# One gather in 4 KB rows, a bounce through DRAM, and free loading at the head of a mixture-of-experts kernel

## What is computed

```python
# x (32, 64, 512), itok (32,), cond_weights (200, 64, 64), E = 8 experts, I = 352
w  = cond_weights[itok]                       # one 64 x 64 matrix per batch entry
xf = einsum('bct,bcd->bdt', x, w).reshape(2048, 512)
gate = softmax(xf @ Wr.T)                     # (2048, 8)
# the two best experts of each row; an expert keeps its first 640 rows
g = silu(xf @ Wg[e].T); u = xf @ Wu[e].T; out_e = (g * u) @ Wd[e].T
y = sum over the two experts of gate * out_e
result = x + y
```

## Time and profile before

| | us |
|---|---|
| median of 3 runs | 307.38 (306.9 to 308.51) |
| the profiled execution, its own time | 307.83 |
| its span in the trace | 306.0 |
| PE busy | 281.3 (92%) |
| DVE, ACT, POOL busy | 134.4, 125.7, 139.1 |

### The profile page before, as it was taken

The page is one execution under the profiler, slowest core; times in us unless marked ns, Lnnn a source line. Parts: engine busy times, 40 slices in busy tenths (PEclk is TensorE's granted clock), DMA queues, the critical chain, the costliest instruction groups (busy, mean ns, idle before and its releaser), DMA issues.

```text
span 306.0 us, 4658 instructions
## 1 busy us (share of the span) xinstructions
PE 281.3 (92%) x1626; PEld 248.0 (81%) x1627; DVE 134.4 (44%) x259; ACT 125.7 (41%) x212; POOL 139.1 (45%) x128
## 2 busy tenths in 40 slices
PE   2899898799989999999999999999999999999940
PEld 2576366699879999999999999999999999999930
DVE  2377895434334344543444355354335534423200
ACT  2132675243334435534354354444435445432220
POOL 5773087500374343545444436454753553454230
PEclk9999995999999999999999999999999999999995
DMA  4855693979796867578658675795879666474422
GB/s 155 277 182 154 249 383 104 327 293 403 266 170 150 215 148 174 163 180 152 149 90 229 131 176 170 161 165 150 238 158 208 157 132 103 69 138 47 58 37 35
DMA packets 24992, 53.17 MB, mean 174 GB/s; under 512 B 3344, under 2 KB 3344, under 8 KB 24976
## 3 DMA queue, kind: packets, MB, share of 16 engines
q0 software_dynamic: 9472, 21.67, 37.4%
q1 hardware_dynamic: 15504, 31.29, 30.7%
HBM read 32.69 MB, written 20.25 MB: 173 GB/s over the span
## 4 chain that ended last, share of the span: by engine, by line
PE 75%; DMA 10%; POOL 5%; DVE 3%; issue 2%; SPq 2%; POOLq 1%; ACT 0%; DVEq 0%
PE bank L853 39%; PE bank L873 21%; PE bank L836 4%; DMA out<-x_sb 4%; DMA tiles<-xf_dram,src_row 4%; PE bank L897 3%; POOL whi L399 3%; PE bank L736 3%; PE bank L748 2%; DMA x_sb<-x 2%; POOL tiles L412 1%; SPq L344 1%; PE bank L771 1%; PE bank L780 1%; PE bank L758 1%
## 5 line engine op out<-in xcount | busy, mean ns | idle before, releaser
L412 POOL DMA_INDIRECT tiles<-xf_dram,src_row x40 | 44.3, 1107 | 95.4 <-ACT tiles L504 65.7
L424 POOL DMA_INDIRECT out<-tiles,dst_row x40 | 66.2, 1654 | 43.7 <-DMA out<-tiles,dst_row 20.1
L853 PE MATMUL bank<-whi,xhi 128*128 128x352 f32 x280 | 73.4, 343 | 0.8 <-ACT xhi L488 0.8
L853 PE MATMUL bank<-wlo,xhi 128*128 128x352 f32 x280 | 67.9, 323 | 0.0
L853 PE MATMUL bank<-whi,xlo 128*128 128x352 f32 x280 | 56.8, 324 | 0.0
L853 PEld LDWEIGHTS bank<-wlo,xhi 128*128 128x128 f32 x280 | 48.8, 188 | 0.0
L696 DVE TENSOR_TENSOR xlo<-bank,xhi 128x512 fp32r<-128x512 f32 x35 | 24.2, 691 | 55.8 <-ACT xhi L488 55.8
L853 PEld LDWEIGHTS bank<-whi,xlo 128*128 128x128 f32 x280 | 47.0, 189 | 0.0
L853 PEld LDWEIGHTS bank<-whi,xhi 128*128 128x128 f32 x280 | 45.7, 189 | 1.2 <-issue 1.2
L488 ACT ACTIVATE xhi<-bank 128x512 fp32r<-128x512 f32 x35 | 21.0, 599 | 61.0 <-PE bank L836 61.0
L873 PE MATMUL bank<-whi,hhi 128*128 128x512 f32 x105 | 41.4, 395 | 1.4 <-DVE hlo L720 1.4
(11 more groups left out here) (92 smaller groups left out, 248.0 us busy)
## 6 DMA issues: line engine op xcount, KB each, us to landing
raw<-wgu SPq DMA_DIRECT2D x32, 352.0 KB, 3.8
x_sb<-x SPq DMA_DIRECT2D x8, 512.0 KB, 4.2
raw<-wd SPq DMA_DIRECT2D x8, 512.0 KB, 3.8
out<-x_sb SPq DMA_DIRECT2D x4, 1024.0 KB, 7.5
xf_dram<-tiles SPq DMA_DIRECT2D x7, 520.0 KB, 4.0
raw<-wd SPq DMA_DIRECT2D x8, 192.0 KB, 5.1
out<-x_sb SPq DMA_DIRECT2D x1, 1280.0 KB, 13.3
tiles<-xf_dram,src_row POOLq DMA_INDIRECT x40, 4.7
```

Of the source, the lines that this page charges most:

```text
L412: nc.gpsimd.indirect_dma_start(out=xg[:, n % TPE, :], out_offset=None, in_=xf_dram[:, :], in_offset=bass.IndirectOffsetOnAxis(ap=src_row[: ...
L424: nc.gpsimd.indirect_dma_start(out=out[:, :], in_=y_sb[:, n % TPE, :], in_offset=None, out_offset=bass.IndirectOffsetOnAxis(ap=dst_row[:, ...
L853: last = nc.tensor.matmul(ps[:, 0:I], left[:, b, c], right[:, half, o:o + I], start=(k == 0 and left is xhi and right is whi), stop=(k == ...
```

## The change

The condition matrices come in one indirect DMA: each 64 x 64 matrix is seen as four rows of 4 KB, a partition takes one of the 128 rows, and DVE makes one column of row numbers. Since the rows land in another layout than the blocks need, ACT's queue writes them to a scratch tensor in DRAM (`wsel_dram`) and reads them back into both diagonal blocks of `wbd` with two DMAs of 64 x 16 pieces of 256 bytes. The copies on DVE and ACT into `wbd` go away. The wait between the loads of x goes away, the router's weights come padded to 32 columns from the host (64 KB, no memset before), and the first expert's weights wait for no gather. PE begins with ten 128x512 bf16 matmuls on zeros. All logits now stand ahead of all wide products; ACT takes tile 15's copy too, and does three copies of xf before its second exponential. Two of the four 1 MB pieces of the initial copy to `out` are issued early.

```diff
@@ SP
-            for half in range(2):
-                sp.dma_start(condb[half * C:(half + 1) * C, :],
-                             cond[half:half + 1, :].broadcast_to([C, TT])).then_inc(cond_in, 16)
             load_x(0)
-            sp.wait_ge(wr_clear, 1)
-            sp.dma_start(wr_sb[:, :, 0:E],
-                         wr.rearrange("(k p) e -> p k e", p=P)).then_inc(wr_in, 16)
+            sp.dma_start(wr_sb[:, :, :], wr[:, :, :]).then_inc(wr_in, 16)
             for m in range(1, TT // 2):
-                if m >= 2:
-                    sp.wait_ge(x_in[m - 2], 16)
                 load_x(m)
...
-            sp.wait_ge(wc_in[NG - 1], 16 * GR)
             sp.wait_ge(pad_ok, 1)
             for u in range(NU):
                 load_unit(0, u)
+            def init_out(q):
+                for m in range(q * XR // 2, (q + 1) * XR // 2):
+                    sp.wait_ge(x_in[m], 16)
+                sp.dma_start(out_t[:, q * XR:(q + 1) * XR, :],
+                             x_sb[:, q * XR:(q + 1) * XR, :]).then_inc(out_init, 16)
+            for q in range(EARLY_OUT):          # EARLY_OUT = 2
+                init_out(q)
...
-            for m in range(TT // 2):
-                sp.wait_ge(x_in[m], 16)
-            for q in range(TT // XR):
-                sp.dma_start(out_t[...], x_sb[...]).then_inc(out_init, 16)
+            for q in range(EARLY_OUT, TT // XR):
+                init_out(q)
@@ POOL
             pool.wait_ge(cidx_ok, 1)
-            for j in range(TT):
-                nc.gpsimd.indirect_dma_start(
-                    out=wc_sb[:, j, :], out_offset=None, in_=wcond[:, :],
-                    in_offset=bass.IndirectOffsetOnAxis(ap=cidx[:, j:j + 1], axis=0),
-                ).then_inc(wc_in[j // GR], 16)
+            nc.gpsimd.indirect_dma_start(
+                out=wsel_sb[:, :], out_offset=None, in_=wcond[:, :],
+                in_offset=bass.IndirectOffsetOnAxis(ap=cidx[:, 0:1], axis=0),
+            ).then_inc(wsel_in, 16)
@@ ACT
-            for j in range(0, TT, 2):
+            act.dma_start(condb[:, :], cond[:, :]).then_inc(cond_in, 16)
+            for j in TURN_ACT:                  # the even tiles and 15
                 act.wait_ge(tT_ps, j + 1)
                 nc.scalar.activation(tT_sb[...], ps_tT[j % XR][...], ACT.Copy)
+                if j == SENT_AT:                # 2
+                    act.wait_ge(wsel_in, 16)
+                    act.dma_start(wsel_dram.rearrange("b (q e) -> (b q) e", q=CQ),
+                                  wsel_sb[:, :]).then_inc(wsel_out, 16)
+                if j == BACK_AT:                # 6
+                    act.wait_ge(wbd_clear, 1)
+                    act.wait_ge(wsel_out, 16)
+                    wsel_t = wsel_dram.rearrange("(j t) (c d) -> t c j d", t=2, d=D)
+                    for t in range(2):
+                        act.dma_start(wbd[t * C:(t + 1) * C, :, t * D:(t + 1) * D],
+                                      wsel_t[t]).then_inc(wbd_in, 16)
             exps(0)
...
-            xf_copy(0, 0)
+            for n in range(XR - 1):
+                xf_copy(n, n)
             exps(1)
-            for n in range(1, XR):
-                xf_copy(n, n)
+            xf_copy(XR - 1, XR - 1)
@@ PE
+            pe.wait_ge(warm_clear, 1)
+            for _ in range(WARM_UP):            # 10
+                nc.tensor.matmul(ps_lg[0][:, :], warm[:, 0:P], warm[:, :], start=True, stop=True)
             pe.wait_ge(consts, IDENT)
...
             def logits(g):
                 pe.wait_ge(xr_ok, g + 1)
-                if g < NG - 1:
-                    pe.wait_ge(wbd_ok, 2 * (g + 1))
-                else:
-                    pe.wait_ge(wbd_last_ok, 2)
+                pe.wait_ge(wbd_in, 32)
```

More of the change, by code:

```diff
@@ L93, in build @@
         carry = sb("carry", [P, E, A])
-        condb = sb("condb", [P, TT], I32)
-        cidx = sb("cidx", [P, TT], U32)
-        wc_sb = sb("wc_sb", [P, TT, D])
+        condb = sb("condb", [P, 1], I32)
+        row_i = sb("row_i", [P, 1], I32)
+        part_i = sb("part_i", [P, 1], I32)
+        part = sb("part", [P, 1])
+        cidx = sb("cidx", [P, 1], U32)
+        wsel_sb = sb("wsel_sb", [P, CP * D])
+        warm = sb("warm", [P, H], BF16)
         wbd = sb("wbd", [P, TT, 2 * D])
@@ L219, in build @@
         out_t = out[0:N, :].rearrange("(j p) h -> p j h", p=P)
+        TURN_ACT = [j for j in range(TT) if j % 2 == 0 or j == TT - 1]
+        TURN_DVE = [j for j in range(TT) if j not in TURN_ACT]
         def tile(i, s):
@@ L357, in _ @@
         def _(pool):
[L359 to L365, removed]
+            nc.gpsimd.iota(row_i[:, :], [[0, 1]], base=0,
+                           channel_multiplier=1).then_inc(consts, 1)
             nc.gpsimd.memset(ident[:, :], 0.0).then_inc(consts, 1)
-            pool.wait_ge(consts, 3)
+            pool.wait_ge(consts, 2)
             nc.gpsimd.affine_select(out=ident[:, :], in_=ident[:, :], compare_op=ALU.not_equal,
@@ L530, in _ @@
         def _(dve):
[L531 to L535, removed]
+            nc.vector.memset(warm[:, :], 0.0).then_inc(warm_clear, 1)
+            dve.wait_ge(consts, 1)
+            nc.vector.tensor_scalar(part_i[:, :], row_i[:, :], CQ - 1, None,
+                                    ALU.bitwise_and).then_inc(part_ok, 1)
+            dve.wait_ge(part_ok, 1)
+            nc.vector.tensor_copy(part[:, :], part_i[:, :]).then_inc(part_ok, 1)
+            dve.wait_ge(part_ok, 2)
+            dve.wait_ge(cond_in, 16)
+            nc.vector.tensor_scalar(cidx[:, :], condb[:, :], float(CQ), part[:, :], ALU.mult,
                                     ALU.add).then_inc(cidx_ok, 1)
             nc.vector.memset(wbd[:, :, :], 0.0).then_inc(wbd_clear, 1)
[L539 to L548, removed]
+            nc.vector.memset(raw[IR:P, DOWN + (KI - 1) * H:WC], 0.0).then_inc(pad_ok, 1)
             chain = [0]
@@ L567, in gates @@
                                         ALU.subtract).then_inc(sub_ok, 1)
+            def gates(h):
+                js = slice(h * HALF, (h + 1) * HALF)
+                wide = [P, HALF, E]
                 dve.wait_ge(ex_ok, h + 1)
@@ L728, in _, with turned @@
         def _(pe):
+            def turned(j):
+                if j in TURN_ACT:
+                    pe.wait_ge(tT_act_ok, TURN_ACT.index(j) + 1)
+                else:
+                    pe.wait_ge(tT_dve_ok, TURN_DVE.index(j) + 1)
             def x_tile_turn(j):
@@ L740, in router @@
             def router(g):
-                pe.wait_ge(tT_even_ok, (g + 1) * (GR // 2))
-                pe.wait_ge(tT_odd_ok, (g + 1) * (GR // 2))
+                for j in range(g * GR, (g + 1) * GR):
+                    turned(j)
                 if g >= 1:
@@ L791, in _ @@
                     x_tile_turn((g + 1) * GR + 1)
+                else:
+                    logits(0)
                 router(g)
@@ L795, in _ @@
                     x_tile_turn((g + 1) * GR + 3)
-                if g == NG - 1:
-                    logits(0)
+                else:
+                    logits(1)
                 turn(g)
-            for g in range(1, NG):
+            for g in range(2, NG):
                 logits(g)
-                condition(g - 1)
-            for j in range(NG - 1, BEFORE_RANKS):
+            for j in range(BEFORE_RANKS):
                 condition(j)
```

73 lines of the change are left out of this document (37 added, 36 removed).

## The result

| | before | changed |
|---|---|---|
| median of 4 runs each, one chip | 307.88 us (306.9 to 308.51) | 322.41 us (322.3 to 323.92) |
| profiled execution, its span | 307.83, 306.0 | 322.3, 320.5 |

The ratio is 1.0494 (1.0451 to 1.0537): the change makes the kernel 4.9% slower, 14.5 us. The forecast was 304.2.

The account below looks back on a forecast made before the run. The prediction took only the start of DVE's second half of gates and one PE stall to move the end: 307.83 - 1.5 (head) - 1.7 (stall) = 304.6, or 304.2 for the median, range 301.3 to 308.0.

Parts of the forecast that it names:

- the second sum: DVE's sum after the second exponential in the head: predicted at L + 8.7, 29.7 us, against 31.23 before.
- the matrices' path: Head: condition numbers, gather, write to scratch, reload; predicted to have the matrices in place at 21.0 us.
- The exponential behind the copies of xf: Head, on ACT: second exponential waits for three copies of xf, predicted to lose 1.4 us.
- The stall: Expert loop: PE's single wait for POOL's sixth gather, behind the initial output copy; all 1.7 us predicted to go.
- L: Time at which PE can start its first logits, the later of two paths; predicted 21, so the head gains 1.5 us.
- fair shares: Rival for the head's transfers, chance 0.20: gather gets half the engines beside x; L = 18.7, time 301.9.
- L to the second sum: Head, from PE's first logits to DVE's sum after the second exponential: predicted 8.7 us.
- the fourth rival: Lower clock over the expert loop's first tile, chance 0.07: about 3 us at half speed, 1.5 lost, time 305.7.
- ACT's DMAs behind SP's backlog: Rival, chance 0.10: queues served in issue order, write and reload each pay 5.4 us more; L = 30, time 313.
- Late matrices: Rival, chance 0.18: gather, write and reload each take the upper price; L = 24.3, time 307.4, no change.
- the main case: The prediction's own sum, chance 0.45: L from 19.5 to 22.5, time from 302.8 to 305.8.
- POOL's 15 other gathers: Head: removing them was predicted to be worth nothing, since they do not stand in the chain.

Follow-up runs that it names:

- b_held: Changed kernel with SP's first weights and early output held until the reload has landed: 308.95 us, ratio 0.967 to the kernel before.
- m_held_again: b_held run again unchanged in the fourth set: 308.96 us, ratio 0.965 to the kernel before.
- after_again: The changed kernel run again unchanged in the second set, on another chip: 321.02 us, ratio 1.003 to the kernel before.
- n_after_third: The changed kernel run again unchanged in the fourth set: 321.95 us, ratio 1.008 to the kernel before.
- h_cond: b_held with the condition numbers issued first on SP's queue instead of on ACT's: 310.62 us, ratio 0.972 to the kernel before.
- f_filled: Changed kernel with 16 and 24 bf16 matmuls on zeros in PE's waits before tile 12's turn and the first logits: 315.78 us, ratio 0.987 to before.
- g_gathers: b_held with 13 more indirect gathers on POOL behind the needed one, into an unread buffer: 318.53 us, ratio 0.997 to the kernel before.
- d_free: Kernel before with x loads unpaced, weights not waiting for the gathers and two output pieces early: 318.53 us, ratio 0.998 to the kernel before.
- before_again: The kernel before run again unchanged in the second set, on another chip: 319.19 us, ratio 1.000.

## Why the prediction was wrong

**What held.** The kernel is bound where the prediction said: the second sum is 14.8 us later than in the earlier trace rows, the end 14.5, and nearly all of it was there before the expert loop. The order of the matrices' path, reload last with PE's first logits right behind it, is that of the chain. The exponential behind the copies of xf costs what was said, 1.4: from the first logits to the second sum are 8.60 us in b_held (24.59 to 33.19) and 7.24 in i_exps (22.97 to 30.21). The stall of the earlier trace rows went, all 1.7 of it. It went with room to spare. POOL's sixth gather in the changed kernel still waits for the output:

```profile
89.48 0.94 POOL L415 DMA_INDIRECT tiles<-xf_dram,src_row  x1 [17.37 <-DMA out<-x_sb]
```

But it lands 3.3 us later, and PE turns its tile only at 100.53. Counted from PE's first tile of the loop it goes out after 20.1 us, before after 27.5: 7.4 us earlier, where the prediction had some 6.

**The step that failed first: the matrices' path to L.** Term by term, with what each measured:

| term | predicted | measured | off |
|---|---|---|---|
| gather issued | 3.8 | 5.84 | +2.0 |
| gather | 7.0 | 7.35 | +0.4 |
| write | 5.0 | 6.15 | +1.2 |
| ACT's two issues, to the second | 0.5 | 0.76 | +0.3 |
| reload, its second DMA | 4.7 | 10.90 | +6.2 |
| L | 21.0 | 31.16 | +10.1 |

The reload was mis-sized. I took 4.7 between an old gather and a 260 KB gather, and priced its small pieces as 2.0 us of data while busy. That price is enough when nothing else is queued: 3.7 and 3.6 us in b_held and m_held_again. It is wrong beside SP's queue, for two reasons that the windows show. No piece of the reload moves before 23.5, 4.1 us after the first of its DMAs was issued (1.5 in b_held, 17.43 to 18.9); the cause of this is open. And from then to 28 the price of a piece is not its own bytes but the 2 KB piece of the other queue that goes between. My reading of the earlier trace rows, 3.6 us for an old gather beside the loads of x, hid this: those gathers ran while SP was paced and held at most two loads ahead. It is the row of another queue's state. The rule of the Trainium skill that the prediction used for fair shares ("DMA: Bandwidth & Descriptors", section "Queues, rings and completion order": engines take the queues in turn, packet by packet) fits the window of 24 to 26 us, 345 against 345, and those of after_again and n_after_third, 352 against 351 and 354 against 348; it does not explain the wait to 23.5. Such counts can't tell how many pieces a turn holds. Where I erred was to make of equal turns equal bytes: the bytes of two pieces are as 1 to 8.

The condition load has the same mistake in small: 4.4 us for 128 pieces of 4 bytes, issued together with 512 KB of x, against the 2.4 of the earlier trace rows, measured when SP had issued it first. In h_cond, first in the queue, it is 2.0 again. But the time saved there is lost in gather and write, so its 2.0 us are in the sum and not in what could be gained.

**The step that failed second: L to the second sum.** Predicted 8.7, measured 14.9. f_filled measures 8.6 with the same order and the same late reload, so the order was right, and what I left out is the clock: 6.2 us to the prediction's 8.7, 6.3 to f_filled. (The order was sized with luck: the prediction's L + 5.2 for the last logits doesn't follow from its own prices, which give 5.45; b_held has 5.1.) The prediction took the full clock in the head for granted once the warm-up had run, and considered the lower one only around the lists. Waits of PE of 3.4 to 3.8 us in the head, which the prediction had at 1 to 2 us, stand ahead of both stretches at 0.50. The clock fell again over the loop's first tiles, as the fourth rival had it, in this window of the changed kernel from 70 to 90:

```profile
70.00:90.00 20.00, 18.11 (x102) 17.21 (x103) 7.48 (x10) 5.93 (x12) 2.32 (x3) 0.91 0.94 340
```

A mean of 0.91 over 20 us is 3.6 us at 0.50, if the rest is at 1.00; the stretch lies at 71.5 to 74.9. What remains for it in the sum below is about 1.0 us; no run took it apart.

**The sum as it came out.** L is 10.1 later than predicted, the way to the sum 6.2 longer: second sum at 46.05 instead of 29.7, and 14.8 behind the earlier trace rows. From there to the loop 0.8 more than before (23.3 against 22.5; the wait for the first gather is 1.6, before 0.8), the first tile 1.0 more, the stall 1.7 less: 14.9. PE's last down products start at 304.54, before at 289.64: 14.9.

**The rivals.** ACT's DMAs behind SP's backlog had the side and the place, at 0.10. Its mechanism, service in the order of issue, would have made write and reload alike, 9.4 each; they took 6.15 and 10.90, and from 24 on the windows show turns, not order. From 20.2 to 23, where SP's queue alone moves, they would allow it, so it is refuted as a whole and not for that part. Its L of 30 was nearly right; its time of 313 was not, mainly because it too left the clock out. Late matrices, at L = 24.3, fell short; fair shares and the main case are refuted by L. That POOL's 15 other gathers are worth nothing, as the prediction had it, held for the first chip alone. On the four others the kernel before loses some 11.5 us of its head to them, and the change, which has one gather, does not: so it costs 4.9% on one chip and 0.3 to 0.8% on two others. (Of the four, two have a trace of a kernel with the 16 gathers, one a trace of g_gathers, one only its times.) The trace of the first chip could not tell this.

**A better version.** i_exps, the change with weights and early output held until the reload has landed and the exponential first, takes 307.21, 3.8% less than the kernel before on its chip (3.5 to 4.2) and some 4.5% less than the changed kernel takes on others (321.0 to 322.0). It was not run on a chip where the kernel before takes 307.9; whether it wins there stays open. By its second sum, 30.21 against the 31.23 of the earlier trace rows, it would by my estimate be about level or 1 us ahead.

## What to carry to other kernels

Before a transfer that others wait for is put beside bulk loads, count its pieces: in the windows here two queues advanced piece for piece, so the reload's 256-byte pieces got an eighth of the bytes that the 2 KB pieces beside them got, and most of them moved only when the bulk was through. Hold the bulk until the chain's transfers have landed (one wait, 13 us here), and price a DMA only from a row with the same queues filled. And when a change lets PE wait for some us in the head, price the work behind the wait at half the clock as well, or fill the wait with matmuls (6 us here). Expect the lower clock elsewhere too: two traces have 3 us of it behind 9 to 10 us of busy PE.

## What was unexpected of the hardware

DVE can stand still while POOL issues indirect DMAs one after the other: 13 us in three waits beside 16 of them, one of 7.8 us beside 14, on three chips by their traces (d_free, before_again, g_gathers), and on four of five, as it seems, by the time of the kernel before. The column of the granted clock reads 1.00 at the start of the kernel while matmuls run at half speed: eight passes of a router product take 1.94 us at 12.61 in the kernel before, and 1.06 at 17.22. And a DMA issued with nothing ahead of it in its own queue can move nothing at first: the reload, issued at 19.44 and 20.12, got no packet through from 20.2 to 23, while SP's queue moved 1.08 MB of its remaining 2.8.
